# A spectral layer's inverse transform on one core: the products over row and column frequencies cut into smaller TensorE tiles

## The chip, the core and the metric

The kernel runs on one core of a Trainium2 chip. The metric is the device time of one execution in microseconds (us), from launch to end. A core has five engines that run side by side and meet at semaphores: TensorE (PE in the profile; the loading of its stationary operand is listed as PEld), VectorE (DVE), ScalarE (ACT), GpSimd (POOL) and SyncE (SP), which here issues the DMA transfers. TensorE writes to PSUM only, which has 8 banks of 512 fp32 values on each of 128 partitions; DVE and ACT move results from there to SBUF.

## What is computed

Sixteen images of 32 channels and 64x64 pixels pass through four layers, each normalised over groups of channels and added to its input: a 3x3 convolution, a gated recurrence over the 64 columns, a spectral product of 16x16 modes, and a spectral product of all modes.

```python
x = x + _L0_conv_ref(_gn(x), L0_conv_weight, L0_conv_bias)
x = x + _L1_conv_ref(_gn(x), ...)
x = x + _L2_conv_ref(_gn(x), L2_conv_w_real, L2_conv_w_imag)
x = x + _L3_conv_ref(_gn(x), L3_conv_kernel_re, L3_conv_kernel_im, L3_conv_bias)

def _L3_conv_ref(x, kernel_re, kernel_im, bias):
    kernel = kernel_re + 1j * kernel_im
    x_ = jnp.fft.rfftn(x, s=DIMS).astype(kernel.dtype)
    y_ = jnp.einsum('oihw,bihw->bohw', kernel, x_)
    y = jnp.fft.irfftn(y_, s=DIMS)
    return y + bias
```

The change lies in the last step, the inverse transform `irfftn` of 16 images x 32 channels to 64x64 pixels, with the bias and the residual added.

## The kernel before

The image stays in SBUF (`image`). The stages follow one another: convolution (to about 120 us), recurrence (to about 320 us), forward transform (to about 404 us), the two spectral products (to about 513 us; the second, line L828, is called the mixing stage here) and the inverse transform (to the end). All matrices of the transforms are constants in `kept` and `matrices`.

The inverse transform goes over four groups of four images. On TensorE a group has three parts, and the code's order of them is the order of their execution:

- `back_transposes` (L898): 32 transposes of 128x128 turn the spectrum of the *next* group so that row frequencies lie on partitions. ACT and DVE copy the 8 banks into `by_kh` (helper line L306, six on ACT and two on DVE).
- the product over row frequencies (L909 in `back`): 8 banks of 4 matmuls. The stationary operand is a 128x128 piece of `by_kh`, and its columns, four images x 32 column frequencies, become the partitions of the result. The moving operand is the matrix `ih` with 128 columns: real and imaginary part x 64 rows. `move_kh` then copies each pair of banks to `by_kw` in pieces of 64 partitions (helper `to_kw`, L405): a piece holds two images and one part, and goes to the partitions of that part. ACT has the first two images, DVE the last two, with 8 copies each in a group.
- the last product, over column frequencies (L925): 8 banks of 4 matmuls with 128x128 pieces of `by_kw` (partitions: part, image of a pair, frequency) against `iw` of 128 columns, in which two blocks side by side belong to the two images, with zeros elsewhere. `add_result` on DVE (L1569) adds bias and residual for half a bank, 128x256, at a time: 16 instructions in a group.

All 8 PSUM banks serve all three parts, so each part waits for the banks that the one before it used: `b_act` and `b_dve` say that L909's banks are copied, `a_act` and `a_dve` that the transposes' banks are, `image_done` that L925's are added, and `b_done` and `c_done` report the products' banks to the copying engines. The order on TensorE is: transposes of group 0; then for each group j the product over rows of j, the transposes of j+1 (not for the last), the last product of j. Groups 1 and 2 run as two passes of a hardware loop; groups 0 and 3 are written out. On ACT a group is `move_kh(j)` and the copies of the transposes of j+1; on DVE `move_kh(j)`, two copies of transposes, `add_result(j)`. SP writes a group's images out when all its `image_done` are in, and the last group's in four bands (L480).

An fp32 matmul call appears in the trace as two matmul and two weight-load records, a transpose as one of each.

Of the kernel before, what the change touches and what calls it, by code (L numbers as in the profile page):

```python
# [16 lines left out]
ACT = mybir.ActivationFunctionType  # L17
# [4 lines left out]
P = HM * C  # L22
# [5 lines left out]
GB = 4  # L28
# [13 lines left out]
def constants():  # L42
# [29 lines left out]
    iw = np.concatenate([np.kron(np.eye(2), back_r), np.kron(np.eye(2), back_i)])  # L72
# [4 lines left out]
KEPT_COLS = dict(ident=P, ih=P, iw=2 * W)  # L77
# [3 lines left out]
def program(nc, x, conv_w, conv_b, scan_wi, scan_wh, scan_b, w2, w3, w9, out_b, group_d, const_d, out):  # L81
    ctx = ExitStack()
    with ctx:
# [168 lines left out]
        c_done, image_done = sem("c_done"), sem("image_done")  # L252
        stored = sem("stored")
# [146 lines left out]
        def to_kw(copy, k, x_, ri, *func):  # L400


            src = psum[H * x_:H * x_ + H, 2 * k:2 * k + 2, :].rearrange("p n (o r h e) -> p (n o) r h e", o=4, r=2, e=2)[:, :, ri]
            dst = by_kw[H * ri:H * ri + H, :].rearrange("p (x h o e) -> p x o h e", x=2, o=C, e=2)[:, x_, 8 * k:8 * k + 8]
            return copy(dst, src, *func)  # L405
# [5 lines left out]
        def _(sp):  # L411
# [61 lines left out]
            with sp.Fori(0, NG - 1) as j:  # L473
                sp.wait_ge(image_done, j * 16 + 16)
                sp.dma_start(out[:, ds(j * (GB * ROWS), GB * ROWS)], images(j)).then_inc(stored, 16)
            last = (NG - 1) * GB * ROWS
            for i in range(4):
                sp.wait_ge(image_done, (NG - 1) * 16 + 4 * (i + 1))
# [139 lines left out]
        def _(pe):  # L618
# [261 lines left out]
            def back_transposes(j, first):  # L880
# [9 lines left out]
                for i_, n in enumerate(T_ORDER if first else range(8)):  # L890
                    if first and i_ == 2:
                        pe.wait_ge(y_moved, NCHUNK)
                    if not first and n % 2 == 0:
                        pe.wait_ge(b_act, j * 8 + (n - 6))
                        pe.wait_ge(b_dve, j * 8 + (n - 6))
# [3 lines left out]
                    last.then_inc(a_done, 1)  # L899

            def back(j, first, last_group=False):
# [3 lines left out]
                for n in range(8):  # L905
                    if not first:
                        pe.wait_ge(image_done, j * 16 + (2 * n - 14))
                    for i in range(4):
                        last = mm(psum[:, n, P * i:P * i + P], kh[:, :, 2 * n + i // 2, i % 2], cm["ih"],  # L909
                                  start=True, stop=True)  # L910
# [3 lines left out]
                pe.wait_ge(b_act, j * 8 + 8)  # L914
                pe.wait_ge(b_dve, j * 8 + 8)
                for n in range(8):
                    if not last_group:
                        if n in BY_DVE:
                            pe.wait_ge(a_dve, j * 2 + (3 + BY_DVE.index(n)))
                        else:  # L920
                            pe.wait_ge(a_act, j * 6 + (7 + BY_ACT.index(n)))
                    for i in range(2):
                        for x_ in range(2):
                            at_ = 256 * i + 128 * x_
# [697 lines left out]
```

## Time and profile before

| what | value |
|---|---|
| median of three runs | 597.79 us (596.89 to 597.91) |
| the profiled execution | 597.76 us |
| its span, from first to last instruction | 595.9 us |
| mean granted TensorE clock | 0.988 of full |
| inverse transform, first matmul of L909 to the end | 518.45 to 595.9 us |
| one group in it (L909, L898, L925) | 7.54 + 3.60 + 7.54 us |

Busy time of an engine is the time in which it had at least one instruction in work. The chain that ended last is read from the end backwards: each piece waited for the one ahead of it in the list. Matmuls overlap, so the count of records in a stretch says more than their durations.

### The profile page before, as it was taken

How to read it: one execution, taken by the hardware profiler on the slowest of the kernel's cores; microseconds unless marked ns; L12 is line 12 of the kernel's file. 1: busy time of each engine (PE TensorE's matmuls, PEld its weight loads, DVE VectorE, ACT ScalarE, POOL GpSimd, SP SyncE). 2: the span in 40 equal slices, each digit the busy share in tenths (PEclk: the TensorE clock that was granted, in tenths of full speed). 3: DMA queues.
4: the chain of work that ended last, by engine and by line, in shares of the span. 5: the costliest groups of instructions: out<-in, count | busy, mean ns of one | idle time of the engine just before them, and what ended most of it. 6: DMA issues, size and time to landing. Idle time of an engine off the chain costs nothing.

```text
span 595.9 us, 26842 instructions
## 1 busy us (share of the span) xinstructions
PE 539.8 (91%) x10404; PEld 429.0 (72%) x10404; DVE 492.0 (83%) x1273; ACT 396.7 (67%) x897; POOL 311.3 (52%) x425
## 2 busy tenths in 40 slices
PE   3999999699999999999999999988889778999996
PEld 2333333477777777777777999987577667899995
DVE  7778977479989898989898787798899999377876
ACT  3445879767777776777778966676378966756441
POOL 7665654156666666666665302035799799121000
PEclk9999999899999999999999999999999997999999
DMA  6900000011111111111113100003158775003324
GB/s 226 383 6 0 2 2 4 14 39 44 40 40 44 38 41 44 36 44 40 40 44 103 50 2 0 0 2 85 60 151 248 213 227 158 31 1 142 141 123 159
DMA packets 21284, 45.69 MB, mean 77 GB/s; under 512 B 5104, under 2 KB 15600, under 8 KB 20352
## 3 DMA queue, kind: packets, MB, share of 16 engines
q1 hardware_dynamic: 20160, 44.97, 24.2%
q8 instruction: 25, 0.41, 0.3%
q10 hardware_dynamic: 672, 0.15, 0.1%
q0 software_dynamic: 416, 0.07, 0.1%
q14 instruction: 11, 0.09, 0.0%
HBM read 28.53 MB, written 8.39 MB: 62 GB/s over the span
## 4 chain that ended last, share of the span: by engine, by line
DVE 40%; PE 36%; issue 14%; ACT 6%; DVEq 2%; DMA 1%; SPq 0%; ACTq 0%
PE psum L655 8%; DVE spec L1352 8%; DVE work L338 7%; DVE spec L1344 6%; DVE spec L1355 5%; PE psum L770 5%; PE psum L909 5%; PE psum L925 5%; PE psum L786 4%; DVE small L1237 3%; PE psum L898 3%; PE psum L754 2%; ACT work L295 2%; PE psum L828 2%; DVE spec L1347 2%
## 5 line engine op out<-in xcount | busy, mean ns | idle before, releaser
L690 PE MATMUL psum<-spec,matrices 128*32 128x128 f32 x3024 | 110.0, 279 | 14.4 <-ACT spec L1016 7.5
L690 PEld LDWEIGHTS psum<-spec,matrices 128*32 128x32 f32 x3024 | 76.5, 110 | 46.6 <-ACT spec L1016 46.5
L531 POOL TENSOR_TENSOR spec<-spec 64x128 f32<-64x128 f32 x126 | 70.6, 560 | 72.1 <-DVE spec L1355 72.1
L697 PE MATMUL psum<-spec,matrices 128*32 128x128 f32 x3024 | 107.4, 274 | 0.7 <-DMA spec<-work 0.6
L697 PEld LDWEIGHTS psum<-spec,matrices 128*32 128x32 f32 x3024 | 85.6, 111 | 3.7 <-issue 3.6
L828 PE MATMUL psum<-work 128*32 128x128 f32 x2368 | 74.8, 281 | 14.8 <-ACT work L350 10.2
L655 PE MATMUL psum<-spec,matrices 128*64 128x512 f32 x384 | 86.4, 607 | 1.1 <-ACT spec L950 1.1
L828 PEld LDWEIGHTS psum<-work 128*32 128x32 f32 x2368 | 65.7, 113 | 23.7 <-issue 22.2
L338 DVE TENSOR_TENSOR work<-spec,psum 32x512 f32<-32x512 f32 x108 | 73.5, 681 | 3.8 <-PE psum L828 0.5
L509 POOL TENSOR_SCALAR spec<-image,small 32x960 f32<-32x960 f32 (+1 forms) x48 | 55.5, 1157 | 34.6 <-PE psum L655 22.0
L525 POOL TENSOR_TENSOR image<-image,spec 128x128 f32 (+1 forms) x128 | 69.4, 542 | 0.0
L655 PEld LDWEIGHTS psum<-spec,matrices 128*64 128x64 f32 x384 | 27.1, 139 | 53.8 <-issue 50.7
L350 ACT ACTIVATE work<-work 32x256 f32<-32x256 f32 x111 | 46.0, 414 | 14.7 <-DVE work L338 12.4
L1352 DVE SCALAR_TENSOR_TENSOR spec<-spec,work 128x128 f32<-128x128 f32 x126 | 54.5, 432 | 0.5 <-ACT spec L1025 0.3
L338 POOL TENSOR_TENSOR work<-spec,small 32x512 f32<-32x512 f32 x36 | 45.9, 1276 | 14.7 <-DVE small L1445 6.7
L950 ACT ACTIVATE spec<-image,small 96x1024 f32<-96x1024 f32 (+1 forms) x32 | 39.6, 1236 | 19.0 <-PE psum L655 17.5
L1029 ACT ACTIVATE psum<-spec 128x128 f32<-128x128 f32 x126 | 35.5, 282 | 23.5 <-DVE spec L1347 17.3
L1347 DVE SCALAR_TENSOR_TENSOR spec<-psum,small,spec 128x128 f32<-128x128 f32 x126 | 44.3, 351 | 4.5
L1025 ACT ACTIVATE spec<-psum 128x128 f32<-128x128 f32 x126 | 34.9, 277 | 17.1 <-PE psum L690 17.0
L1021 ACT ACTIVATE spec<-psum 128x128 f32<-128x128 f32 x126 | 35.0, 278 | 15.5 <-PE psum L690 10.0
L1237 DVE BATCH_NORM_STATS2 small<-image 128x6 f32<-128x512 f32 x64 | 40.1, 682 | 4.4 <-DMA image<-x_dram 3.3
L405 ACT ACTIVATE work<-psum 64x512 f32<-64x512 f32 x32 | 24.4, 762 | 29.0 <-PE psum L909 28.6
(154 smaller groups left out, 935.5 us busy)
## 6 DMA issues: line engine op xcount, KB each, us to landing
work<-w_dram SPq DMA_DIRECT2D x33, 512.0 KB, 4.2
spec<-work SPq DMA_DIRECT2D x124, 64.0 KB, 1.9
image<-x_dram SPq DMA_DIRECT2D x3, 2048.0 KB, 11.7
out_dram<-image SPq DMA_DIRECT2D x3, 2048.0 KB, 6.3
image<-x_dram SPq DMA_DIRECT2D x4, 512.0 KB, 5.8
work<-w_dram SPq DMA_DIRECT2D x1, 2048.0 KB, 7.7
out_dram<-image SPq DMA_DIRECT2D x4, 512.0 KB, 2.9
kept<-const_dram SPq DMA_DIRECT2D x1, 192.0 KB, 5.5
```

What stands on the lines that cost most here:

```text
L338: return multiply(dst, src, scale, ALU.mult)
L350: return activation(d[:, :, 0, m, :], d[:, :, 2, m, :], ACT.Copy, scale=-1.0)
L509: nc.gpsimd.tensor_scalar(to, of, sc0[j % 2][q, u:u + 1], sh0[j % 2][q, u:u + 1], ALU.mult, ALU.add).then_inc(norm_pool, 1)
L525: nc.gpsimd.tensor_tensor(col, col, state[h].unsqueeze(2), ALU.add).then_inc(added[h], 1)
L531: nc.gpsimd.tensor_tensor(straddled(h, ROWS_01, 0), *of, ALU.subtract).then_inc(lower_ready[h], 1)
L655: last_mm = mm(psum[o, n % 4, :], cv[:, kx, o], rows_[:, 8 * half:8 * half + 8, kx:kx + W], start=kx == 0, stop=kx == 2)
L690: last = mm(psum[QUARTERS[hm], 4 * h + g, 0:HB], sv[:, g, QUARTERS[hm]], moving[hm], start=starts, stop=True)
L697: last = mm(psum[q, 4 * h + g, 0:HB], sv[:, 3 + g, q], e, start=True, stop=stops)
L828: last = mm(o, wt[:, t, r, :], pl[:, t, from_:to], start=starts and k == 0 and r == 0, stop=r == 1, skip_group_check=True)
L1237: v.bn_stats(bnv[:, at_:at_ + 6], image[:, ds(j * (GB * ROWS) + 512 * k, 512)]).then_inc(half_sem, 1)
L1347: v.scalar_tensor_tensor(out=pre2[h], in0=psum[:, 4 * h + 2, 0:HB], scalar=bias_s[:, 2:3], in1=pre1[h], op0=ALU.add, op1=ALU.add).then_inc ...
L1352: v.scalar_tensor_tensor(out=keep[h], in0=gz[h], scalar=1.0, in1=columns[:, ds(w * (2 * HB) + h * HB, HB)], op0=ALU.subtract, op1=ALU.mult ...
```

## The change

The product over row frequencies is issued in tiles with 32 stationary columns: for each channel and each pair of images, four matmuls with 64 moving columns, one for each (image, part), which write to the four quarters of the partitions (`over_kh`). So a result bank has (image of the pair, part, column frequency) on its partitions for 8 channels, and one pair of images: a bank moves to `by_kw` in one copy of 128 partitions, even banks on ACT, odd ones on DVE. The matmul calls of this part go from 32 to 256 in a group.

The last product works on 64 partitions (one image: both parts x 32 frequencies) and 64 stationary columns: four matmuls with 64 moving columns, two for each image, where one with 128 stood (`over_kw`). The matrix `iw` has 64 columns and no zero blocks, stored twice. The two images of a pair go to the two banks of a pair; so `c_done` comes once for two banks, and `add_result` takes whole banks, 128x512, in 8 instructions. Calls: from 32 to 128 in a group. The semaphore `kw_begun` is counted up ahead of each pair of banks by TensorE's queue, and nothing waits for it.

```diff
--- before.py
+++ after.py
@@ -69,12 +69,12 @@
     back_r = cos[kw] * scale
     back_i = -sin[kw] * scale
     back_i[0] = 0.5 * (-1.0) ** np.arange(W) / (H * W)
-    iw = np.concatenate([np.kron(np.eye(2), back_r), np.kron(np.eye(2), back_i)])
+    iw = np.tile(np.concatenate([back_r, back_i]), (2, 1))
     parts = dict(ident=ident, fw=fw.reshape(P, -1), fh=fh.reshape(P, -1), ih=ih, iw=iw)
     return group.astype(np.float32), {k: v.astype(np.float32) for k, v in parts.items()}
 
 
-KEPT_COLS = dict(ident=P, ih=P, iw=2 * W)
+KEPT_COLS = dict(ident=P, ih=P, iw=W)
 FORWARD_COLS = dict(fw=4 * PADK, fh=2 * H)
 
 
@@ -250,6 +250,7 @@
         a_done, a_act, a_dve = sem("a_done"), sem("a_act"), sem("a_dve")
         b_done, b_act, b_dve = sem("b_done"), sem("b_act"), sem("b_dve")
         c_done, image_done = sem("c_done"), sem("image_done")
+        kw_begun = sem("kw_begun")
         stored = sem("stored")
 
 
@@ -397,11 +398,12 @@
 
         T_ORDER = (4, 6, 0, 2, 5, 7, 1, 3)
 
-        def to_kw(copy, k, x_, ri, *func):
-
-
-            src = psum[H * x_:H * x_ + H, 2 * k:2 * k + 2, :].rearrange("p n (o r h e) -> p (n o) r h e", o=4, r=2, e=2)[:, :, ri]
-            dst = by_kw[H * ri:H * ri + H, :].rearrange("p (x h o e) -> p x o h e", x=2, o=C, e=2)[:, x_, 8 * k:8 * k + 8]
+        def to_kw(copy, n, *func):
+
+
+            k, x_ = n // 2, n % 2
+            src = psum[:, n, :].rearrange("p (o h e) -> p o h e", o=8, e=2)
+            dst = by_kw.rearrange("p (x h o e) -> p x o h e", x=2, o=C, e=2)[:, x_, 8 * k:8 * k + 8]
             return copy(dst, src, *func)
 
 
@@ -471,11 +473,11 @@
                     slot = (i + 1) % 4
                     sp.dma_start(w3_m[slot], w3[:, ds(q * 4096 + i * 1024, 1024)]).then_inc(w3_in[slot], 16)
             with sp.Fori(0, NG - 1) as j:
-                sp.wait_ge(image_done, j * 16 + 16)
+                sp.wait_ge(image_done, j * 8 + 8)
                 sp.dma_start(out[:, ds(j * (GB * ROWS), GB * ROWS)], images(j)).then_inc(stored, 16)
             last = (NG - 1) * GB * ROWS
             for i in range(4):
-                sp.wait_ge(image_done, (NG - 1) * 16 + 4 * (i + 1))
+                sp.wait_ge(image_done, (NG - 1) * 8 + 2 * (i + 1))
                 band = [t[:, last:last + GB * ROWS].rearrange("p (b i m) -> p b i m", b=GB, i=4)[:, :, i] for t in (out, image)]
                 sp.dma_start(band[0], band[1]).then_inc(stored, 16)
             sp.wait_ge(stored, 16 * (NG + 3))
@@ -891,39 +893,62 @@
                     if first and i_ == 2:
                         pe.wait_ge(y_moved, NCHUNK)
                     if not first and n % 2 == 0:
-                        pe.wait_ge(b_act, j * 8 + (n - 6))
-                        pe.wait_ge(b_dve, j * 8 + (n - 6))
+                        pe.wait_ge(b_act, j * 4 + (n // 2 - 3))
+                        pe.wait_ge(b_dve, j * 4 + (n // 2 - 3))
                     b, g = n // 2, n % 2
                     for i in range(4):
                         last = nc.tensor.transpose(psum[:, n, P * i:P * i + P], src[:, g, :, :, i, b], cm["ident"])
                     last.then_inc(a_done, 1)
 
+            def over_kh(n, o):
+
+
+                c, x_ = 8 * (n // 2) + o, n % 2
+                for q in range(4):
+                    b_, r = 2 * x_ + q // 2, q % 2
+                    last = mm(psum[KW * q:KW * q + KW, n, H * o:H * o + H], kh[:, KW * b_:KW * b_ + KW, c // 2, c % 2],
+                              cm["ih"][:, H * r:H * r + H], start=True, stop=True)
+                return last
+
+            def over_kw(n, i, x_):
+
+
+                at_ = W * (4 * x_ + 2 * (n % 2) + i)
+                for b_ in range(2):
+                    rows_ = slice(H * b_, H * b_ + H)
+                    for o in (slice(0, P // 2), slice(P // 2, P)):
+                        last = mm(psum[o, n - n % 2 + b_, at_:at_ + W], kwv[rows_, x_, n, i, o], cm["iw"][rows_],
+                                  start=True, stop=True)
+                return last
+
             def back(j, first, last_group=False):
 
                 pe.wait_ge(a_act, j * 6 + 6)
                 pe.wait_ge(a_dve, j * 2 + 2)
                 for n in range(8):
-                    if not first:
-                        pe.wait_ge(image_done, j * 16 + (2 * n - 14))
-                    for i in range(4):
-                        last = mm(psum[:, n, P * i:P * i + P], kh[:, :, 2 * n + i // 2, i % 2], cm["ih"],
-                                  start=True, stop=True)
+                    if not first and n % 2 == 0:
+                        pe.wait_ge(image_done, j * 8 + (n - 6))
+                    for o in range(8):
+                        last = over_kh(n, o)
                     last.then_inc(b_done, 1)
                 if not last_group:
                     back_transposes(j + 1, False)
-                pe.wait_ge(b_act, j * 8 + 8)
-                pe.wait_ge(b_dve, j * 8 + 8)
+                pe.wait_ge(b_act, j * 4 + 4)
+                pe.wait_ge(b_dve, j * 4 + 4)
                 for n in range(8):
-                    if not last_group:
-                        if n in BY_DVE:
-                            pe.wait_ge(a_dve, j * 2 + (3 + BY_DVE.index(n)))
-                        else:
-                            pe.wait_ge(a_act, j * 6 + (7 + BY_ACT.index(n)))
+                    if not last_group and n % 2 == 0:
+                        for k in (n, n + 1):
+                            if k in BY_DVE:
+                                pe.wait_ge(a_dve, j * 2 + (3 + BY_DVE.index(k)))
+                            else:
+                                pe.wait_ge(a_act, j * 6 + (7 + BY_ACT.index(k)))
+                    if n % 2 == 0:
+                        pe.sem_inc(kw_begun, 1)
                     for i in range(2):
                         for x_ in range(2):
-                            at_ = 256 * i + 128 * x_
-                            last = mm(psum[:, n, at_:at_ + 128], kwv[:, x_, n, i], cm["iw"], start=True, stop=True)
-                    last.then_inc(c_done, 1)
+                            last = over_kw(n, i, x_)
+                    if n % 2 == 1:
+                        last.then_inc(c_done, 1)
 
             back_transposes(0, True)
             back(0, True)
@@ -1161,9 +1186,8 @@
 
             def move_kh(j):
                 for k in range(4):
-                    act.wait_ge(b_done, j * 8 + (2 * k + 2))
-                    for ri in range(2):
-                        to_kw(a, k, 0, ri, ACT.Copy).then_inc(b_act, 1)
+                    act.wait_ge(b_done, j * 8 + (2 * k + 1))
+                    to_kw(a, 2 * k, ACT.Copy).then_inc(b_act, 1)
 
 
             yv = ystage.rearrange("p (n b) -> p n b", b=GB)
@@ -1556,16 +1580,15 @@
             def move_kh(j):
                 for k in range(4):
                     dve.wait_ge(b_done, j * 8 + (2 * k + 2))
-                    for ri in range(2):
-                        to_kw(v.tensor_copy, k, 1, ri).then_inc(b_dve, 1)
+                    to_kw(v.tensor_copy, 2 * k + 1).then_inc(b_dve, 1)
 
             def add_result(j):
 
-                for n in range(8):
-                    dve.wait_ge(c_done, j * 8 + (n + 1))
-                    for i in range(2):
-                        part = images(j).rearrange("p (b h w) -> p h b w", b=GB, w=W)[:, 2 * n + i]
-                        res = psum[:, n, 256 * i:256 * i + 256].rearrange("p (b w) -> p b w", b=GB)
+                for k in range(4):
+                    dve.wait_ge(c_done, j * 4 + (k + 1))
+                    for b_ in range(2):
+                        part = images(j).rearrange("p (x b h w) -> p b h x w", x=2, b=2, w=4 * W)[:, b_, k]
+                        res = psum[:, 2 * k + b_, :].rearrange("p (x w) -> p x w", x=2)
                         v.scalar_tensor_tensor(out=part, in0=res, scalar=bias_o[:, 0:1], in1=part,
                                                op0=ALU.add, op1=ALU.add).then_inc(image_done, 1)
```

On TensorE, in the looped copy of a group, the product over row frequencies stood like this before (`kept` holds `ih` and `iw`, `work` holds `by_kh` and `by_kw`; the first two banks are shown, and the numbers are partitions x columns of the result):

```order
L907 ISA [waits a_dve]
L909 MATMUL psum<-kept,work 128x128 [waits image_done]
L909 MATMUL psum<-kept,work 128x128 x3
L907 REGISTER_ALU
L909 MATMUL psum<-kept,work 128x128 [waits image_done]
L909 MATMUL psum<-kept,work 128x128 x3
```

and so it stands now (the first two pairs of banks):

```order
L930 ISA [waits a_dve]
L909 MATMUL psum<-kept,work 32x64 [waits image_done]
L909 MATMUL psum<-kept,work 32x64 x63
L930 REGISTER_ALU
L909 MATMUL psum<-kept,work 32x64 [waits image_done]
L909 MATMUL psum<-kept,work 32x64 x63
```

Eight times as many calls stand in the same place, with one wait for `image_done` for two banks instead of one for each. The last product in the same loop, before, with its first two banks:

```order
L921 REGISTER_ALU [waits b_dve,b_act]
L925 MATMUL psum<-kept,work 128x128 [waits a_act]
L925 MATMUL psum<-kept,work 128x128 x3
L921 REGISTER_ALU
L925 MATMUL psum<-kept,work 128x128 [waits a_act]
L925 MATMUL psum<-kept,work 128x128 x3
```

and now, with its first two pairs:

```order
L944 REGISTER_ALU [waits b_dve,b_act]
L944 REGISTER_ALU [waits a_act]
L920 MATMUL psum<-kept,work 64x64 [waits a_act]
L920 MATMUL psum<-kept,work 64x64 x31
L942 REGISTER_ALU
L944 REGISTER_ALU [waits a_dve]
L920 MATMUL psum<-kept,work 64x64 [waits a_act]
L920 MATMUL psum<-kept,work 64x64 x31
```

The waits for the copies of the transposes are the same, taken for two banks at a time. On DVE a group is now four copies of 128 partitions, two copies of transposes and eight additions, in the order as before. Nothing else moves on the other engines.

## Rows read from the trace of the kernel before

**Rows 1.** The page: span, and busy time and instructions by engine.
```profile
span 595.9 us, 26842 instructions
PE 539.8 (91%) x10404; PEld 429.0 (72%) x10404; DVE 492.0 (83%) x1273; ACT 396.7 (67%) x897; POOL 311.3 (52%) x425
```

**Rows 2.** Chain that ended last, 505 to 596 us: start us, us, what.
```profile
by line: PE psum L909 33.4%; PE psum L925 33.4%; PE psum L898 16.5%; PE psum L828 6.4%; DVE work L405 1.6%; ACT work L350 1.4%; ACT work L306 1.3%; issue 0.9%; DVE work L338 0.8%; DVE image L1569 0.5%; DVEq L83 0.4%
...
518.45 7.80 PE psum L909 x64
526.25 3.60 PE psum L898 x32
529.85 7.54 PE psum L925 x64
537.39 7.54 PE psum L909 x64
...
574.74 7.55 PE psum L909 x64
...
583.91 7.79 PE psum L925 x64
...
591.73 0.48 DVE image L1569
```

**Rows 3.** Stretches: length, busy time (records) by engine, clock, DMA.
```profile
core 0: us, PE busy (x) PEld busy (x) DVE busy (x) ACT busy (x) POOL busy (x), PEclk, DMA share, GB/s
537.23:544.76 7.53, 7.53 (x66) 7.53 (x65) 5.59 (x9) 4.53 (x6) 0.00 (x0) 1.00 0.66 279
544.76:548.36 3.60, 3.60 (x35) 3.60 (x33) 3.10 (x4) 3.35 (x6) 0.00 (x0) 1.00 0.00 0
548.36:555.90 7.54, 7.54 (x67) 7.54 (x65) 5.89 (x14) 1.61 (x4) 3.60 (x1) 1.00 0.01 2
```

**Rows 4.** Groups by line and shape, 518 to 596 us.
```profile
L405 ACT ACTIVATE work<-psum 64x512 f32<-64x512 f32 x32 | 24.4, 762 | 29.0 <-PE psum L909 28.6
L405 DVE COPY work<-psum 64x512 f32<-64x512 f32 x32 | 24.1, 754 | 9.6 <-PE psum L909 9.1
L1569 DVE SCALAR_TENSOR_TENSOR image<-psum,small,image 128x256 f32 x48 | 21.0, 480 | 5.2 <-PE psum L925 3.8
L306 ACT ACTIVATE work<-psum 128x512 f32<-128x512 f32 x19 | 10.6, 683 | 0.1
L306 DVE COPY work<-psum 128x512 f32<-128x512 f32 x6 | 4.4, 739 | 0.8 <-PE psum L898 0.7
```

**Rows 5.** Timeline of PE at 346 us: start us, us, line, operation, records.
```profile
345.54 0.99 PE L786 MATMUL psum<-matrices,work 128*128 128x128 f32 x7
346.45 0.46 PE L798 MATMUL psum<-matrices,work 128*32 128x32 f32 x32
```

**Rows 6.** Line L798, all its matmuls: duration ns min/median/max, first and last start.
```profile
L798 PE MATMUL psum<-matrices,work x128: 196/196/221, 346.5 to 403.6; 128*32 128x32 f32 x128
```

**Rows 7.** One stretch of line L828 in the mixing stage, columns as in rows 3.
```profile
506.90:508.90 2.00, 1.96 (x64) 1.69 (x64) 1.28 (x2) 1.77 (x4) 1.17 (x2) 1.00 0.53 199
```

**Rows 8.** The page: two groups by line, count, busy us, mean ns.
```profile
L828 PE MATMUL psum<-work 128*32 128x128 f32 x2368 | 74.8, 281 | 14.8 <-ACT work L350 10.2
L1347 DVE SCALAR_TENSOR_TENSOR spec<-psum,small,spec 128x128 f32<-128x128 f32 x126 | 44.3, 351 | 4.5
```

**Rows 9.** Timeline, 582 to 596 us, columns as in rows 5.
```profile
582.31 1.45 DVE L405 COPY work<-psum 64x512 f32<-64x512 f32 x2 [0.37 <-PE psum L909]
583.91 7.78 PE L925 MATMUL psum<-kept,work 128*128 128x128 f32 x64 [1.64 <-DVE work L405]
585.13 7.47 DVE L1569 SCALAR_TENSOR_TENSOR image<-psum,small,image 128x256 f32<-128x256 f32 x16 [1.37 <-PE psum L925]
586.98 6.04 SPq L480 DMA_DIRECT2D out_dram<-image  x4
```

**Rows 10.** The page: instruction fetches on queue 8: packets, MB, share of 16 engines.
```profile
q8 instruction: 25, 0.41, 0.3%
```


## The prediction

> **What bounds the kernel now.** The change touches only the last 77 us, so I went from the page's busy times [rows 1] straight to the chain that ended last in that stretch [rows 2]. There the reader is to see that TensorE's three parts follow one another without a gap: L909, L898, L925, together 83% of the chain from 505 us on, and no copy stands between them except once at the start and once in the last group. One group is the distance of two like pieces: (574.74 - 537.39) / 2 = 18.68 us. The stretches of one group [rows 3] confirm it from the other side: PE is busy in all of 7.53, 3.60 and 7.54 us, DVE in 5.6, 3.1 and 5.9, ACT in 4.5, 3.4 and 1.6, at clock 1.00. So in a steady group only TensorE's time counts; DVE has 4 us to spare and ACT 9. In the tail, the last group [rows 9], it is otherwise: no transposes cover the wait for the copies, and the last addition and the output follow.
>
> **The copies.** ACT had 8 of 762 ns a group and DVE 8 of 754 [rows 4]; now each has 4 on 128 partitions and as many elements on each. The nearest rows are the transposes' copies, 128x512, 683 and 739 ns [rows 4]. So each engine gets about 3 us a group back. In groups 0 to 2 that is worth nothing, because TensorE is the chain. In the tail two copies of 1.45 us together become one of 0.74.
>
> **The product over row frequencies.** 256 calls are 512 matmul records a group in place of 64. What does one cost? The full-size ones follow each other every 7.54 / 64 = 0.118 us [rows 2]. For tiles with 32 stationary columns the trace has two sizes, each with the four quarters in turn as here. With 128 moving columns, L828: 64 records in 1.96 us [rows 7], the last of them 0.28 long [rows 8], so (1.96 - 0.28) / 63 = 26.7 ns apart. With 32 moving columns, L798: 32 records in 0.46 us [rows 5], the last 0.196 [rows 6], so 8.5 ns apart. The four quarters thus work side by side, and the price goes with the moving columns. 64 columns lie a third of the way: 8.5 + 18.2 / 3 = 14.6 ns, and 512 of them 7.5 us, as much as before. The bounds are the two rows themselves, 4.4 us (all as at 32 columns) and 13.7 us (nothing saved by the shorter moving operand). I take 14.6, because between these rows time is bought by columns.
>
> The TensorE page of the Trainium skill ("TensorE: Matmul & The Clock Gate", section "Wait — 56ns, not 53.3ns?") speaks against this: matmuls start no closer than about 25 ns apart, however few columns. Row L798, with 8.5 ns, disagrees for four tiles in turn. By the page the 512 would take 12.8 us.
>
> **The last product.** 128 calls, 256 records in place of 64, each with 64 moving columns on one of four 64x64 tiles. The trace has no tile with fewer than its full rows, so this is bounded. Below: four tiles at once, 256 x 14.6 ns = 3.7 us; the full-size row gives the same, half the columns and a quarter of the array, 0.118 / 2 / 4 = 14.7 ns. Above: the two row halves take turns, twice that, 7.5 us, what it costs now; all four in turn would be 15 us, but L828's quarters exclude that for the column halves. I take 3.8 us, since the two halves read other partitions, write to other banks (b_ picks the bank), and the zero blocks of `iw`, half of the old work, are gone.
>
> **Changes of tile shape.** From L786 to L798 [rows 5]: seven full records from 345.54, 0.118 apart, would let the next start at 346.37; L798 starts at 346.45. So 0.08 us a change, three in a group: 0.25.
>
> **Waits, group by group.** A group becomes 7.5 + 3.6 + 3.8 + 0.25 = 15.2 us. Does anything now come late for it? DVE's additions double their size: 351 ns for 128 elements [rows 8] and 480 for 256 [rows 4] give 0.74 for 512; 8 of them 5.9 us against 16 at 7.47 / 16 = 0.47, that is 7.5 [rows 9]. DVE's group is 4 x 0.74 + 2 x 0.74 + 5.9 = 10.3 us, ACT's 10 copies of 0.68 are 6.8: both below 15.2. TensorE's first waits fall on `image_done`: the last pair of banks is reported 3.8 us after the last product begins and added in four steps of 1.5 us from its first pair on (1.2 us in), so by 7.1 us; the next group's product needs that pair at 3.9 + 0.75 x 7.5 = 9.5 us. Behind these waits stand all later matmuls, so a miss would cost its full size; there are 2.4 us of room. `over_kw` waits for six ACT copies of the transposes, the first two done about 2 us after the transposes begin and needed at 3.6. The copies of the row product end 1 us after it, and the transposes need the last pair's banks 2.7 us after it. GpSimd's 3.60 us of `ystage` [rows 3] have 11 us. SP's stores follow `image_done` and lie beside everything. `kw_begun` is a queue instruction that no one waits for; I put it at nothing, hidden by matmuls already queued, and 0.1 us a group if they run out.
>
> **Instruction fetches.** TensorE's program grows. A looped group was 4 x 64 + 2 x 32 = 320 instructions (four to a call, two to a transpose) and is now 4 x 384 + 64 = 1,600. Before, 25 packets of 16.4 KB were fetched, 0.3% of 16 engines' span: 0.003 x 16 x 595.9 = 28.6 us, 1.1 us each [rows 10]. Written out, the program had 6,358 instructions (1,474 calls of four, 192 transposes of two, 78 others), so a packet holds about 256. So a group now eats 6.25 packets, one in 2.4 us. A transfer of 1.1 us fits under that if it is asked for early. I add one exposed packet, 1.1 us, for the jump back of the loop, bounds 0 and 4.
>
> **The tail and the sum.** Group 0's L909 starts at 518.45, as before. Three groups of 15.2 us and 0.26 for the first matmul's length (7.80 against 7.54, [rows 2]) bring the last row product to 564.3 and its end to 571.8 (582.29 before). One copy, 0.02 + 0.74, and 0.15 until TensorE goes on (582.31 + 1.45 to 583.91, [rows 9]): 572.7. First pair of banks 0.94, its report 0.28 (1.22 to the first addition for 0.94 of matmuls, [rows 9]): 573.9. Then DVE is the chain, 8 x 0.74 = 5.9: 579.8. From the last addition to the end 3.3 us (585.13 + 7.47 to 595.9): 583.1. With the packet 584.2, plus 1.9 outside the span (597.76 - 595.9): 586.1 us. The profiled execution is within 0.03 us of the median of the runs.
>
> **Rivals.**
> 1. *The row halves take turns* in the last product: nothing in the rows speaks against it directly. The group is 18.9 us, the last row product ends at 582.9, the last product at 591.6, the last addition at 593.1: 598.2 us, no change. 11%.
> 2. *Instructions run short* (slower). Place: the straight run of 1,024 instructions of `over_kh` behind the loop's jump. If each packet is asked for only when the one ahead of it is used up, 1.1 us is exposed each time: 12.5 packets (second pass and last group) give 585.0 + 13.8 = 598.8, all 25 give 612.5. From 0.5 us exposed per packet on, the change loses. For it: no stretch before used a packet in less than about 4 us (128 instructions in 1.96 us, [rows 7]). Against: the matmuls of L828 wait for no fetch there. 8%, near 605.
> The Trainium skill, "Runtime: NRT & Kernel Launch", section "Instruction fetch mechanics", says that TensorE holds 128 KiB of instructions as a FIFO of 16 KiB blocks filled ahead, and that a taken branch to a block no longer held waits for a fetch. The 16.4 KB of a packet agree; by its figure the looped group, 100 KB, just fits or just misses.
> 3. *A price per matmul*, whatever its columns (slower): 26.7 ns as at L828. Products of 13.7 and 6.8 us, a group of 24.4, the end at 620. L798 speaks against it, but it is a burst of 32 records, and these are runs of 512 and 256. 5%. By the TensorE page's 25 ns the time would be about 615.
>
> **Chances and range.** My own case, four tiles at once and fetches mostly covered, has 73%; its own range is 583 to 591 (3.7 to 4.2 us for the last product, 7.3 to 8 for the other, 0 to 4 us of fetching). Between it and rival 1 (halves that overlap in part) I put 3%. The range to 598.5 takes in rival 1 and the mildest of rival 2. A measurement of this kernel tells 0.2%, 1.2 us, from no change. Faster 76%, same 11%, slower 13%.
>
> **What would show it.** Right: L909 at 512 and L920 (the last product) at 256 records a group, in about 7.5 and 3.8 us; no PE idle between parts; ACT copies at 0.68, DVE additions at 0.74; DVE alone at the end of the chain. Wrong: L920 at 7.5 us (rival 1); PE idle with "issue" named, above all behind the loop's jump, and 40 fetches on queue 8 close to the gaps (rival 2); L909 near 13 us with no idle (rival 3); PE waiting for `image_done` (my room of 2.4 us misjudged).

## The result, and the profile after

The changed kernel takes 617.05 us (614.74 to 618.25), the kernel before 597.58 us on the same chip: a ratio of 1.0323, 95% interval 1.0294 to 1.0352. It is slower, and far above the range, which the prediction ends at 598.5. The profiled execution took 618.01 us, 616.2 of them in the span.

The first view to open is the same as before: the chain that ended last. Its pieces are start us, us, what.

```profile
by line: PE psum L909 32.0%; issue 24.0%; PE psum L920 15.2%; PE psum L900 14.3%; PE psum L830 5.2%; DVE image L1592 1.8%; ACT work L307 1.1%; ACT work L351 0.7%; DVE work L407 0.6%; DVEq L83 0.6%
...
517.51 2.21 PE psum L909 x141
519.72 1.43 issue
521.15 1.99 PE psum L909 x122
523.14 1.74 issue
524.88 1.99 PE psum L909 x128
526.88 2.02 issue
528.89 3.04 PE psum L909 x115
...
547.51 5.39 issue
552.89 5.61 PE psum L909 x255
...
571.02 7.36 PE psum L909 x512
578.38 3.81 PE psum L900 x32
582.18 4.24 PE psum L920 x256
...
592.26 5.58 issue
597.84 4.71 PE psum L909 x199
```

Before, "issue" was 0.9% of this chain [rows 2]; now it is 24.0%. L909 is the row product, L900 the transposes, L920 the last product. Two things are to be seen. In the group from 571.02 on (the second pass of the loop) there is no gap, and the prices are close to the forecast: 7.36 us for 512 records (14.4 ns each), 4.24 us for 256 (16.6 ns). In the other three groups TensorE stops, as a rule, after every 128 matmul records. A matmul record goes with one weight load, so that is every 256 instructions, one packet of [rows 10]. Most of these gaps last 1.4 to 2 us; two last more than 5.

The stretches of the four groups and, inside group 1, those around the gap at 547.5 (columns as in [rows 3]):

```profile
517.50:542.20 24.70, 17.79 (x800) 16.75 (x800) 8.37 (x13) 7.72 (x11) 3.60 (x1) 0.93 0.02 4
542.20:571.00 28.80, 18.41 (x807) 17.20 (x800) 9.50 (x14) 5.91 (x10) 3.60 (x1) 0.88 0.19 77
571.00:586.40 15.40, 15.38 (x804) 15.11 (x808) 8.60 (x14) 6.04 (x10) 0.00 (x0) 1.00 0.33 136
586.40:616.20 29.80, 13.99 (x771) 13.00 (x768) 10.57 (x16) 2.61 (x4) 0.00 (x0) 0.86 0.39 144
...
547.51:552.89 5.38, 0.00 (x0) 0.00 (x0) 0.00 (x0) 0.16 (x1) 0.00 (x0) 0.72 0.38 158
552.89:556.20 3.31, 3.31 (x124) 3.31 (x128) 0.69 (x1) 0.50 (x1) 0.00 (x0) 0.50 0.02 5
556.20:558.50 2.30, 2.30 (x142) 2.02 (x132) 0.69 (x1) 0.55 (x2) 0.00 (x0) 0.90 0.04 7
```

The held group takes 15.40 us against 18.68 before; the others take 24.7, 28.8 and 29.8 (the last with the tail). Behind the long gap the granted clock is 0.50, the lower of TensorE's two levels, and 124 records take 3.31 us where 128 took 1.99. So a gap can cost twice: once as idle time, and once more at half clock. That was so behind both long gaps, and once behind the third of three short ones (528.89 to 531.93, mean granted clock 0.57).

The groups by line (columns as in [rows 4]), and the queue of the instruction fetches:

```profile
L909 PE MATMUL psum<-kept,work 128*32 128x64 f32 x2029 | 35.7, 235 | 20.8 <-issue 20.8
L920 PE MATMUL psum<-kept,work 64*64 64x64 f32 x1024 | 18.2, 223 | 6.3 <-issue 5.4 <-DVE work L407 0.9
L1592 DVE SCALAR_TENSOR_TENSOR image<-psum,small,image 128x512 f32 x24 | 16.3, 745 | 6.6 <-PE psum L920 6.6
L407 DVE COPY work<-psum 128x512 f32<-128x512 f32 x16 | 11.1, 692 | 42.7 <-PE psum L909 42.7
L407 ACT ACTIVATE work<-psum 128x512 f32<-128x512 f32 x16 | 10.3, 642 | 55.5 <-PE psum L909 55.5
...
q8 instruction: 40, 0.66, 0.4%
```

The bulk of the 33 us by which the span misses the forecast (616.2 against 583.1 without the packet) can be added up on the chain. The 14 "issue" pieces of at least 0.1 us from 517.5 on sum to 26.2 us. The pieces that ran at less than full clock (528.89, 531.93, 552.89, 597.84) took 5.5 us more than their records cost in the held group. The row product began 0.94 us earlier than before (517.51 against 518.45), which leaves 2.3 us that I have not followed.

### The profile page after: what moved, and what is told of

The parts are those of the page before. It is cut to its first block, busy times and chain, and to the rows that moved or that the text cites. A ratio compares the mean times of both kernels' runs of the same rounds, so it can differ in the third digit from the quotient of the medians.

```text
span 616.2 us, 31881 instructions
## 1 busy us (share of the span) xinstructions
PE 532.5 (86%) x12964; PEld 419.9 (68%) x12964; DVE 471.9 (77%) x1225; ACT 382.4 (62%) x881; POOL 311.4 (51%) x425
## 4 chain that ended last, share of the span: by engine, by line
DVE 38%; PE 34%; issue 16%; ACT 5%; POOL 3%; DVEq 2%; DMA 1%; POOLq 0%; SPq 0%; ACTq 0%
DVE spec L1376 8%; PE psum L657 8%; PE psum L909 6%; DVE work L339 6%; DVE spec L1368 6%; DVE spec L1379 5%; PE psum L772 5%; PE psum L788 4%; DVE small L1261 3%; PE psum L920 3%; PE psum L900 3%; PE psum L756 2%; POOL work L339 2%; ACT work L296 2%; PE psum L830 2%
## 5 line engine op out<-in xcount | busy, mean ns | idle before, releaser
L830 PE MATMUL psum<-work 128*32 128x128 f32 x2368 | 73.7, 278 | 14.6 <-ACT work L351 11.6
L909 PE MATMUL psum<-kept,work 128*32 128x64 f32 x2048 | 35.9, 235 | 21.5 <-issue 20.8
L339 POOL TENSOR_TENSOR work<-spec,small 32x512 f32<-32x512 f32 x36 | 46.3, 1285 | 15.2 <-DVE small L1469 6.7
L909 PEld LDWEIGHTS psum<-kept,work 128*32 128x32 f32 x2048 | 33.7, 121 | 23.5 <-issue 22.2
```

The costliest lines, as they stand in the source:

```text
L339: return multiply(dst, src, scale, ALU.mult)
L830: last = mm(o, wt[:, t, r, :], pl[:, t, from_:to], start=starts and k == 0 and r == 0, stop=r == 1, skip_group_check=True)
L909: last = mm(psum[KW * q:KW * q + KW, n, H * o:H * o + H], kh[:, KW * b_:KW * b_ + KW, c // 2, c % 2], cm["ih"][:, H * r:H * r + H], start= ...
```

## The experiments

All times stand against the kernel before on the same chip, 596.6 to 597.2 us. Three explanations were put up. A: after each 256 instructions TensorE pauses for a fixed time. B: instructions arrive at a fixed pace of 256 for every 3.5 to 3.75 us, and TensorE stops when its work for them is shorter. C: the small tiles, or image and part on partitions, are slow in themselves.

**Streams behind the kernel's own work (m1_streams).** The changed kernel, with matmuls of one kind added behind its last store, so that nothing else runs:

```
            def call(c, n):
                q = c % 4
                return mm(psum[KW * q:KW * q + KW, c // 4 % 8, 0:n], kh[:, KW * q:KW * q + KW, 0, 0],
                          cm["ih"][:, 0:n], start=True, stop=True)
...
            for c in range(256):
                call(c, 32)
```

Behind these 32-column calls follow 256 with 64 columns, 256 with 128, a loop of 8 passes of 64 calls with 64 columns, and 256 with 64 columns beside a 2 MB store, with full-size matmuls between.

> Adds, behind the changed kernel's own work and after its last store, five streams of matmuls on TensorE, four 32-column tiles in turn: 512 records written out with 32 moving columns, with 64, with 128; then 8 passes of a hardware loop of 128 records with 64; then 512 written out with 64 while 2 MB are stored once more. Theory A (a new block of 256 instructions costs TensorE's queue a fixed pause of about 2.1 us when it is first run, of which the 64 instructions already queued hide some): gaps every 128 records; period 1.1 + 1.8 = 2.9 us at 32 columns, 1.85 + 1.8 = 3.7 at 64, 3.4 + 1.2 = 4.6 at 128; in the loop 14.3 ns a record without gaps after the first pass; one gap of 5 to 6 us in the last stream. Theory B (instructions come at a steady pace of 256 in 3.75 us): 3.75 us for 128 records at each width, the loop free of gaps. Theory C (small tiles are slow by themselves): 29 ns a record in the loop too, and no gaps that keep to 256 instructions.

The total, 724.55 us, says nothing. Timeline of PE (start us, us, line, operation, records, idle before):

```profile
631.94 1.39 PE L965 MATMUL psum<-kept,work 128*32 128x32 f32 x128 [2.12 <-issue]
635.40 1.94 PE L965 MATMUL psum<-kept,work 128*32 128x32 f32 x128 [2.06 <-issue]
638.85 0.80 PE L965 MATMUL psum<-kept,work 128*32 128x32 f32 x42 [1.52 <-issue]
...
646.87 2.55 PE L965 MATMUL psum<-kept,work 128*32 128x64 f32 x166
650.69 2.00 PE L965 MATMUL psum<-kept,work 128*32 128x64 f32 x128 [1.28 <-issue]
654.15 2.00 PE L965 MATMUL psum<-kept,work 128*32 128x64 f32 x128 [1.46 <-issue]
657.88 1.50 PE L965 MATMUL psum<-kept,work 128*32 128x64 f32 x90 [1.73 <-issue]
...
664.86 14.35 PE L965 MATMUL psum<-kept,work 128*32 128x128 f32 x512
...
684.69 15.70 PE L965 MATMUL psum<-kept,work 128*32 128x64 f32 x1024
...
716.16 6.36 PE L965 MATMUL psum<-kept,work 128*32 128x64 f32 x235 [5.31 <-issue]
```

With 32 columns TensorE resumes 3.46 and 3.45 us after the resumption before, with 64 columns 3.46 and 3.73, though the work between differs. With 128 columns a packet's work lasts 14.35 / 4 = 3.59 us, and there is no gap at all. So A falls and B holds, in the main: the pace is nearly, not quite, fixed. The same 64-column calls in a short loop run 1,024 records in 15.70 us without a gap, so C falls for the tiles. A store beside the stream makes a gap of 5.31 us.

The trace also holds each transfer of the fetch queue, q8, and these show where the pace comes from. Two windows, 631.94 to 632.9 us and 632.9 to 634.0:

```profile
DMA packets 0, 0.00 MB, mean 0 GB/s; under 512 B 0, under 2 KB 0, under 8 KB 0
...
q8 instruction: 1, 0.02, 5.5%
```

The packet moves from 632.98 to 633.94. So its transfer begins 1.04 us after TensorE has resumed at 631.94, in the packet before it, and takes 0.96 us; 1.46 us after it has landed TensorE resumes, at 635.40. That is the 3.46 us. In the four such rounds of the first two streams the three parts are 1.04 to 1.14, 0.96 to 1.30 and 1.29 to 1.46 us, and no transfer for a later packet begins in between.

**The row product alone (e1_row_only).** The row product in 32-column tiles with its copies of 128 partitions, as in the change (the quarters in the order part, image); the last product full-size as before, with a block-diagonal `iw` for two images.

> Only the row product in 32-column tiles (quarters in the order part, image), with its copies of 128 partitions; last product, its matrix and the additions as in the kernel before. By theory A or B the row product, 256 calls, carries nearly the whole loss: 14 to 18 us in groups 0, 1 and 3, 7.4 in group 2 (second pass of the loop), the last product 7.5 as before: 597.6 + 25 = 618 to 625 us. By theory C the row product is as slow in group 2 as elsewhere. If the 64x64 tiles of the last product were the cause, this one would be at 597 or below.

618.1 us, ratio 1.0361 (1.0338 to 1.0384). The row product alone costs all that the change costs: it has gaps in groups 0, 1 and 3 and takes 7.35 us in group 2. What the new last product saves where its code is held, it loses to its own fetches elsewhere.

**The same layout with half as many matmuls (e5_row_64).** As e1, but two images by 32 frequencies in one 64-column tile:

```diff
-                for q in range(4):
-                    b_, r = 2 * x_ + q % 2, q // 2
-                    last = mm(psum[KW * q:KW * q + KW, n, H * o:H * o + H], kh[:, KW * b_:KW * b_ + KW, c // 2, c % 2],
+                for r in range(2):
+                    last = mm(psum[H * r:H * r + H, n, H * o:H * o + H], kh[:, H * x_:H * x_ + H, c // 2, c % 2],
```

> The last product, additions and stores as before the change; the row product keeps the changed layout (image and part on partitions), but in 64-column tiles: two images times 32 frequencies in one matmul, 128 calls (256 records, 512 instructions) a group in place of 256 (512 records). Theory B (instructions arrive at a steady 256 for every 3.5 to 3.75 us, whatever they do): 128 records of 64 columns keep TensorE busy for about as long as their instructions take to arrive, so the row product takes 7.4 to 7.9 us in every group, with waits of some tenths of a microsecond between, and the total is 597 to 602 us, beside 618 for the run with 32-column tiles. Theory C (it is the tile shape or the new placement on partitions that is slow, not the count of instructions): the row product loses as much as with 32-column tiles, 612 us or more. If the copies (0.74 us, one for each channel pair and image pair) or their waits carried the loss, the total would stay near 618 too.

597.45 us, ratio 1.0004 (0.9992 to 1.0016). Chain of e5, group 1:

```profile
536.81 7.83 PE psum L906 x256
544.65 3.80 PE psum L899 x32
548.45 7.54 PE psum L933 x64
```

Placement, copies and additions of e1 are all there, the gaps are gone, and so is the whole loss of 21 us. A packet's work is now 7.83 / 2 = 3.92 us, more than nearly all of the intervals seen. With m1 this run settles the cause: against e1 only the tile width was changed, and with it the number of instructions, and m1's loop shows that narrow tiles cost nothing extra where their code is held.

**The stores moved to the end (e2_late_store).** SP waits for all additions before the stores of groups 0 to 2 (`sp.wait_ge(image_done, NG * 8)`).

> The changed kernel with the stores of groups 0 to 2 held back until all additions are done; 6 MB more to store at the end, so the time is some 15 us longer and only the gaps count. If a store that has just been issued makes the two long gaps (5.4 and 5.6 us, each 3 us after a store), both fall to 1.5 to 2.2 us like the others. If they come from something at these places of the program, they stay.

630.87 us, with 6 MB still to store after the last addition. Where the changed kernel had gaps of 5.39 and 5.58 us, the timeline of PE now has these:

```profile
550.07 1.99 PE L909 MATMUL psum<-kept,work 128*32 128x64 f32 x127 [1.82 <-issue]
...
592.26 1.99 PE L909 MATMUL psum<-kept,work 128*32 128x64 f32 x128 [1.74 <-issue]
```

So the long gaps come with a 2 MB store. The changed kernel's queues say how, in the windows 545.5 to 550.4 us and 550.4 to 551.4 (TensorE had resumed at 545.51):

```profile
q1 hardware_dynamic: 127, 1.84, 89.9%
...
q8 instruction: 1, 0.02, 5.5%
```

In the first window only the store's queue, q1, moves anything. The fetch begins at 550.45, 4.94 us after TensorE's resumption instead of about 1.1, and then takes no longer than others, 0.88 us. At the second long gap it begins 5.24 us after, at 595.50, and takes 0.95. So the fetch is not slow; it starts late, when the store is all but through.

**Three groups as passes of one loop (e3_loop3).** `with pe.Fori(0, NG - 1) as j: back(j, False)` in place of a written-out group 0 and a loop of two.

> The changed kernel with group 0 no longer written out: groups 0, 1, 2 are three passes of the one loop, group 3 as it was. Same matmuls in the same order. Theory A and B with code that stays resident: first pass 23 to 25 us, second and third 15.4 each without gaps, group 3 as before the edit: about 604 to 606 us against 617. Theory C, or a supply that also limits code already run: no change, 617.

630.38 us, ratio 1.0561 (1.0534 to 1.0588): a miss. The second pass had no gap (8.98, 3.87 and 4.31 us, the first at low clock), but the third stopped again, with gaps of 4.50 and 6.38 us at its start. The body is about 1,620 instructions, 6.3 packets. The trace has no fetch between 540.04 and 560.39 us, where the second pass runs, and one after another from there on.

**How long a body stays held (m2_loops).** Loops of four passes behind the last store, with bodies of 64 calls (128 records, 256 instructions) times 2, 4, 5, 6 and 7:

> The changed kernel, and behind its last store five loops of four passes each on TensorE, with bodies of 2, 4, 5, 6 and 7 times 256 instructions (64 calls of four 64-column matmuls... 128 instructions for every 64 records; 256 records a body block of 512 instructions). The output is that of the changed kernel; the time is longer by the added work and says nothing. Held theory: passes after the first take their matmul time alone (about 15 ns a record), with no gaps, for as long as the whole body is held on the core; a body that is too long shows gaps again in its third pass, or in every pass, as the run with three passes of the group did with a body of some 1,620 instructions. Rival (the third pass there stopped for another reason: the store or the copies): no loop here has gaps after its first pass, since nothing else runs.

(The parenthesis there counts wrongly: 64 calls are 128 records and 256 instructions, so the bodies are 2, 4, 5, 6 and 7 packets.) Timeline of PE, the loop of 6 from its last gap on, and the start of the loop of 7:

```profile
756.88 33.76 PE L961 MATMUL psum<-kept,work 128*32 128x64 f32 x2367 [1.47 <-issue]
...
816.62 1.77 PE L961 MATMUL psum<-kept,work 128*32 128x64 f32 x112 [1.48 <-issue]
821.84 0.65 PE L961 MATMUL psum<-kept,work 128*32 128x64 f32 x16 [3.45 <-issue]
824.82 5.47 PE L961 MATMUL psum<-kept,work 128*32 128x64 f32 x256 [2.32 <-issue]
```

Up to 6 packets only the first pass has gaps (in the loop of 6, the last 2,367 of 3,072 records run through, and from 759.0 to 790.5 us no DMA queue moves a packet); with 7 every pass has them, the longest where the loop jumps back. That fits e3, whose 6.3 packets lie between the two, but not its clean second pass, which stays open.

The Trainium skill, "Runtime: NRT & Kernel Launch", section "Instruction fetch mechanics", says that a taken branch to a target outside the current window of two pages has to wait for a fetch (the prediction leaves the two pages out). The loop of 7 agrees that a jump back can wait; the loops of 4, 5 and 6 packets, longer than two pages, do not agree with that window. The prediction's figure from this section, 128 KiB, is 8 packets; a body of 7 was not held. The same section says that the next block is fetched while the present one is executed, mostly hidden. That only the next one is fetched agrees with the first runs of records above (x166 in m1: the rest of a packet and one more); that it is hidden does not where a packet holds less work than it takes to come, 1.99 us against 3.45 to 4.0.

**Looking for a version that wins.** A body of at most 6 packets could be held for all four groups. A last product in tiles of 64 rows and 128 columns has half as many matmuls:

```diff
-                    for o in (slice(0, P // 2), slice(P // 2, P)):
-                        last = mm(psum[o, n - n % 2 + b_, at_:at_ + W], kwv[rows_, x_, n, i, o], cm["iw"][rows_],
-                                  start=True, stop=True)
+                    last = mm(psum[:, n - n % 2 + b_, at_:at_ + W], kwv[rows_, x_, n, i], cm["iw"][rows_],
+                              start=True, stop=True)
```

It was run in the changed kernel (e6_last_128), with a loop over all four groups (e7_loop4_128) and with a loop over three (e8_loop3_128):

> The changed kernel, with the last product in tiles of 64 rows and all 128 columns: an image's 64 rows for weights of 128 columns, 64 calls (128 records, 256 instructions) a group in place of 128 (256 records, 512 instructions); layout, copies, additions and stores as in the changed kernel. Where the code is held (second pass of the loop): the last product takes about 3.8 to 4.3 us if the two row halves work side by side, 7.5 us if they take turns. Theory B (256 instructions for every 3.5 to 3.75 us where they have to be fetched): a group has 5.25 times 256 instructions in place of 6.25, so each of the three groups that are fetched loses 3.5 to 3.75 us less, and the total is 605 to 608 us in place of 617. Theory C (small tiles or the layout are slow in themselves): no more than the difference of one last product, 616 us or more.

> All four groups as passes of one loop, with the last product in tiles of 64 rows and 128 columns, so that the body is about 5.25 times 256 instructions; the last pass does the transposes of a group that does not exist (3.8 us on TensorE, read by nobody). By the loops of 2 to 7 times 256 instructions, which ran without gaps from the second pass on up to 6 and with gaps in every pass at 7: first pass 19 to 22 us, the other three 15.2 to 15.5 us with no wait for instructions, in all 589 to 593 us, faster than both kernels. Rival: as in the run with three passes (a body of 6.3 times 256), the third and fourth passes stop for instructions again, 604 us or more.

> Three groups as passes of one loop and the last one written out, with the last product in tiles of 64 rows and 128 columns; no work that nobody reads. If the body of 5.25 times 256 instructions stays held: first pass 19 to 22 us, second and third 15.2 to 15.5 us, and the last group, whose 5 times 256 instructions have to be fetched, 17.5 to 20 us plus one copy, in all 592 to 597 us. If the third pass stops for instructions again, 600 us or more.

e6: 621.03 us, ratio 1.0405 (1.0369 to 1.0441). e7: 605.58, 1.0155 (1.0141 to 1.0169). e8: 610.54, 1.0235 (1.022 to 1.0251). Rows of e6's timeline, then two of e7's (second pass):

```profile
577.36 7.75 PE L919 MATMUL psum<-kept,work 64*128 64x64 f32 x128
585.04 2.81 PE L909 MATMUL psum<-kept,work 128*32 128x64 f32 x185
589.19 1.99 PE L909 MATMUL psum<-kept,work 128*32 128x64 f32 x128 [1.34 <-issue]
595.67 5.60 PE L909 MATMUL psum<-kept,work 128*32 128x64 f32 x199 [4.48 <-issue]
```

```profile
543.08 7.35 PE L911 MATMUL psum<-kept,work 128*32 128x64 f32 x512
...
554.16 7.75 PE L921 MATMUL psum<-kept,work 64*128 64x64 f32 x128
```

The loop does what m2 says: passes 2, 3 and 4 of e7 run without a gap, 18.8 us each. But in this shape the row halves take turns: 128 records last 7.75 us, some 60 ns each, half of a full-size record's 118 for half its columns. e6 also missed because I had spread its instructions over the group: the 11.5 us of transposes and last product ahead of 585.04, with 1.25 packets in them, were not used to fetch further ahead. The next row product runs 185 records and stops. Behind its gap of 4.48 us the clock fell, too: the 199 records ran at 0.50, and the last product of that group took 11.66 us at a mean of 0.62 instead of 7.75. e8 shows both again. Its second and third pass have no gap, but its written-out last group has gaps of 1.14 and 4.21 us and a last product of 12.13 us at 0.59.

Two mixtures, a quarter and three eighths of the last product in 64x128 tiles, the rest in 64x64, all groups in the loop:

> All four groups as passes of one loop, as in the last such run, but only a quarter of the last product in tiles of 64 rows and 128 columns (60 ns a record there), the rest in the changed kernel's 64x64 tiles (16.6 ns a record): 224 records a group, a body of 6.0 times 256 instructions and a few waits. If it stays held: last product 3.18 + 1.92 = 5.1 us in passes 2 to 4 in place of 7.7, group 16.2 us, total 605.6 less 3 x 2.6 less about 2 in the first pass, 595 to 597 us, about the kernel before. If a body just over 6 times 256 is too long: gaps from the third pass on, 602 us or more.

> The same with three eighths of the last product in tiles of 64 rows and 128 columns: 208 records a group, a body of 5.9 times 256 instructions. Last product 2.65 + 2.88 = 5.5 us when held, group 16.6 us, total 605.6 less 3 x 2.15 less about 1.7, 596 to 599 us, if the body stays held for all four passes; gaps from the third pass on and 602 us or more if not.

604.51 us, ratio 1.0135 (1.0115 to 1.0155), and 610.15, 1.0251 (1.0198 to 1.0304). Both bodies stay held for all passes, but the last product, here in e9, takes 7.32 us instead of 5.1, and 9.00 in e10 instead of 5.5:

```profile
572.07 7.32 PE L923 MATMUL psum<-kept,work 64*64 64x64 f32 x224
```

e9 changes shape 16 times a group and e10 24 times; 2.2 / 16 and 3.5 / 24 are both about 0.14 us a change. No version that beats the kernel before was found.

## Why the prediction was wrong, step by step

- **Prices of the matmuls: right for the row product, a little low for the last one.** 14.6 and 14.7 ns were forecast; in the held group a row-product record took 14.4 and a last-product record 16.6 (4.24 us against 3.8). Rival 1 was refuted for 64x64 tiles (4.24 us, not 7.5); e6 shows that it would have been true for 64x128. (The trace before does have a tile with fewer than 128 rows, 12 records of 96 rows at L627, but one such tile at a time, so it gives no price for two.) Rival 3, a price for each matmul, fell with m1: 32, 64 and 128 columns cost different work times.
- **Copies, additions, waits: right.** Additions 745 ns against 0.74; copies 692 and 642 against 739 and 683. TensorE waited for `image_done` nowhere on the chain, and the steady group took 15.40 against 15.2 us.
- **"I add one exposed packet, 1.1 us, for the jump back of the loop, bounds 0 and 4": this step failed.** The row behind it [rows 10] gives how long a packet occupies the DMA engines, not how often TensorE gets one. I set 1.1 us against one packet in 2.4 us and called it covered "if it is asked for early". It is not: in m1 the transfer, 0.96 to 1.30 us, is the middle part of a round of 3.45 us or more, which starts when TensorE goes on into the packet before. The runs show one packet for every 3.45 to 4.0 us, and that no more than one is saved up: after 11.5 us of little demand, a run of row product still gets only 128 to 256 records before its first gap (x185 in e6), the rest of the packet in use and one more. The place was wrong as well: behind the loop's jump back 0.22 us was exposed (570.80 to 571.02), and the straight code of the other groups had the rest. The exposed time was 26.2 us in all, not 1.1. The average over a group was the wrong test as well: the row product wants a packet every 1.84 us (7.36 / 4).
- **Rival 2 was the outcome, with too small a chance.** That a fetch is exposed for each packet of `over_kh`, and that its 40 fetches lie close to the gaps, was right. Its place was right only in part: the milder case had the second pass, which was held, and the last group, which was not. Its condition was near (a packet is fetched once the one ahead is begun, not used up), its price of 1.1 us only the transfer's, so near 605 was too mild. The evidence that I held against it, that L828 waits for no fetch, was read wrongly. Its 128 instructions in 1.96 us stand in a loop of 7 passes (`tiles` in the mixing stage), and the trace before has no fetch between 452.67 and 519.61 us; m1's loop shows that held code runs without gaps. It said nothing of straight code, and L798's burst, shorter than a packet, couldn't either.
- **Not in the sum at all:** stores that delay a fetch until the gap is over 5 us (e2 removes this), and the low clock behind gaps (5.5 us).

## What to carry to other kernels

Cutting a matmul into tiles that work side by side keeps TensorE's time and multiplies its instructions; where the code is straight, divide the work of each 256 instructions by the pace at which they arrive (here 3.45 to 4.0 us) before counting any gain. A stretch of a trace that is dense in instructions proves that supply keeps up only if it isn't in a loop whose body is held. Dense code belongs in a loop of no more than some 6 x 256 instructions; quiet time ahead of it buys one packet.

## What the runs showed of the hardware

- TensorE's supply of straight code: 256 instructions every 3.45 to 4.0 us with nothing else running (m1, m2), 6.2 to 7.6 us beside a 2 MB store (e1, the changed kernel, m1). The transfer of a packet begins 1.04 to 1.14 us after TensorE has gone on into the one before (m1), so one packet at most is in reserve; beside the store it begins 4.94 and 5.24 us after.
- A loop body of 6 x 256 instructions, and of 6.0 x 256 with its waits (e9), stays held for four passes; at 7 x 256 every pass refetches. At about 6.3 the second pass ran clean and the third didn't. The second pass made no fetch. Why the third had to is open.
- 64x64 tiles: 16.6 ns a record, four side by side. 64x128 tiles: 60 ns, no overlap of the row halves. A change between the two shapes costs about 0.14 us, an estimate from the last products of e9 and e10.
